# K's edges in four parts, V's image stored inside the column loop, and half of the rotated Q behind the first scores

## The chip, the cores and the metric

The kernel runs on one core of a Trainium2 chip. The metric is the device time of one execution in microseconds, of which the lower is the better; the time of a kernel is the median of several executions. A core has five engines that run their own instruction streams and wait for one another by semaphores: TensorE (PE: matmuls and transposes into PSUM, with weight loads on PEld), VectorE (DVE), ScalarE (ACT), POOL (GpSimd) and SP (SyncE), which here only issues DMAs. PSUM has eight banks of 512 floats in each of 128 partitions.

## The reference

Input x is (1, 128, 40, 40), float32. Cut to what matters:

```
x = x + conv(layernorm over channels of x)          # "conv" is windowed attention, below
t = tokens of x                                     # 1600 x 128
t = t + moe(layernorm(t))                           # t_n + sum of 2 of 8 experts, gelu MLPs 128-128-128

conv(x):  q, k, v = split(x @ w_qkv.T + b_qkv);  q = q / 4;  8 heads of 16 channels
    k_w, v_w = for each pixel its 17 x 17 window of k and of v (zeros outside), C*289 numbers
               per pixel, read as 289 vectors of 128, that is (289, 8 heads, 16)
    attn = softmax(q . k_w) * mask;  out = attn . v_w;  return out @ w_proj.T + b_proj
```

The window's C*289 numbers are laid out channel after channel and then read as 289 rows of 128, so a vector of 16 numbers that a head multiplies with q mostly lies within one channel's window, runs along it, and sometimes crosses from one channel to the next.

## The kernel before

**Stages.** The first 65 us prepare: layernorm, the matmuls for K, Q and V, their images (`kimg`, `vimg`: 40 x 40 with a frame), and several rearranged copies through DRAM. Then comes the column loop (65 to 318 us), one iteration for each of the 40 image columns x, and after it the projection, the router and the experts (318 to 436 us).

**One column.** POOL multiplies the rotated Q with a band (`spread(x)`, into `wb`): these are the weights for `scores(x)` on TensorE, three groups into banks 0 to 2, each of four tiles, against K's turned slab `kt` and its half-swapped copy `kh`. Each group ends with a small matmul that adds the boundary terms `inj` (the vectors that cross channels). VectorE's `shift(x, g)` takes the minimum and adds the mask, ScalarE's `exps(x)` exponentiates, TensorE's `turn_probs(x)` transposes, VectorE's `weigh(x)` masks, TensorE's `products(x)` multiplies with V's skewed slab `sv`, and VectorE's `pick_out(x)`, `pick_sum(x)` take the result. TensorE's iteration i is scores(i), turn_probs(i-1), products(i-2).

**What a column needs made ahead.** VectorE's `turn(x)` makes `kt` for column x from `zt`, in iteration x-2, ScalarE's `half_blocks(x)` the `kh` from it. The boundary terms: POOL's `boundary_mul(x)` multiplies Q (`qb` and `xln`, chunks of four columns, loaded by 15 small DMAs in four groups, `q_load(c, g)`) with `dkx`, VectorE's `boundary_add(x)` sums, POOL's `boundary(x)` spreads to `inj`. In POOL's iteration i the order is spread(i+1), mask(i), boundary_mul(i+3), boundary(i+1). `dkx` is the difference of two pieces of K's image in DRAM: `edges_in` loads them to `gk`, `edge_difference` on VectorE subtracts. V's slab: ScalarE's `slab(x)` copies it from `vimg` to `uv`, SP's `store(x)` writes it to DRAM (484.5 KB), SP's `load(x)` reads it back skewed (539.5 KB) to `sv`. K's four slabs went the same way before the loop: `zslab(n)`, `zk_store(n)`, `zk_load(n)`, then TensorE's `zturn(n)` transposes them, ScalarE's `zt_copy(n)` copies them out. slab(0) and slab(1) use the buffers `uv` that zk_store(2) and (3) read.

**The rotated Q.** `q_turn(k)`, k = 0 to 3, rotates ten columns of Q by 20 small matmuls of 40 columns (the profile counts a float32 matmul as two); `copy_q(k)` on VectorE and `half_of_q(k)` on ScalarE copy the result from bank `QRB[k]` to `qrot` and `qhalf`, which spread(10k) to spread(10k+9) read.

**Order.** All orders are written out by hand, by the code's own order on each engine. SP is one queue: an instruction that waits holds up all behind it.

## Time and profile before

| | us |
|---|---|
| three runs | 436.99, 438.38, 438.93 |
| their median | 438.38 |
| the profiled execution's own time | 437.91 |
| its span | 436.1 |
| busy in it: TensorE | 401.2 (92%) |
| VectorE | 302.0 (69%) |
| ScalarE | 280.2 (64%) |
| POOL | 210.1 (48%) |

The span is the profiled execution from the first to the last instruction; the time has 1.8 us more around it. Busy times are sums over stages that differ in what holds them up, so a share says little about what a change in one stage is worth; the rows below are taken from the stage that is changed. The granted clock of TensorE is 0.945 on the mean of the span.

### The profile page before, as it was taken

To read this page: it belongs to the slowest core of one execution; us is meant where nothing else is said; L and a number is where in the kernel's file an instruction comes from. 1 tells how busy PE (TensorE), PEld (TensorE's weight loads), DVE (VectorE), ACT (ScalarE), POOL (GpSimd) and SP (SyncE) were. 2 spreads that over 40 slices of the span, in tenths; PEclk is the share of its full clock that TensorE was granted. 3 is DMA by queue.
4 is the path that set the end of the run, shared out by engine and by line. 5 is a ranking of instruction groups with operands and counts; after the bars stand their busy time and mean duration, and the time that the engine had idled before them with its cause. 6 is when DMAs were issued, how large, how long until landed. Compare 5 with 4: busy or idle time off the path is not lost.

```text
span 436.1 us, 16839 instructions
## 1 busy us (share of the span) xinstructions
PE 401.2 (92%) x7070; PEld 281.3 (64%) x7070; DVE 302.0 (69%) x765; ACT 280.2 (64%) x495; POOL 210.1 (48%) x268
## 2 busy tenths in 40 slices
PE   4899969599999998999999999999689978999997
PEld 2779955377777676777776776777455544465553
DVE  1351366499999899999988888999465746516323
ACT  2260659698899998999999889677322442253232
POOL 9901161666666565657667667675288030001000
PEclk9695558899999999999999999999899999999999
DMA  6179877866767666566667665446965000000500
GB/s 174 62 245 300 204 210 263 315 197 195 229 209 234 204 213 194 185 219 226 218 173 234 177 213 200 148 158 197 233 217 139 2 0 2 0 20 0 172 19 19
DMA packets 35049, 72.17 MB, mean 165 GB/s; under 512 B 8052, under 2 KB 22029, under 8 KB 34157
## 3 DMA queue, kind: packets, MB, share of 16 engines
q1 hardware_dynamic: 33851, 69.41, 50.2%
q8 instruction: 56, 0.92, 0.9%
q0 software_dynamic: 144, 1.32, 0.8%
q10 hardware_dynamic: 979, 0.36, 0.3%
q14 instruction: 19, 0.16, 0.1%
HBM read 42.24 MB, written 28.84 MB: 163 GB/s over the span
## 4 chain that ended last, share of the span: by engine, by line
PE 77%; DVE 6%; DMA 6%; ACT 5%; issue 3%; SPq 2%; DVEq 0%; ACTq 0%
PE ps L1001 22%; PE ps L1024 10%; PE ps L1046 9%; PE ps L1006 7%; DMA zsl<-uv 5%; PE ps L1165 4%; PE ps L1212 4%; PE ps L1027 3%; PE ps L1032 3%; PE ps L1107 2%; SPq L357 1%; PE ps L1179 1%; PE ps L918 1%; PE ps L1058 1%; DVE prb L1490 1%
## 5 line engine op out<-in xcount | busy, mean ns | idle before, releaser
L1001 PE MATMUL ps<-slabs 128*32 128x401 f32 x528 | 118.2, 512 | 10.5 <-ACT prb L778 4.9
L1001 PE MATMUL ps<-prb,slabs 128*32 128x401 f32 x494 | 114.0, 515 | 0.6 <-issue 0.6
L1413 DVE CUSTOM_DVE_ANT_0 scn<-ps,con 128x401 f32<-128x401 f32 x120 | 65.0, 571 | 21.8 <-PE ps L1006 21.5
L787 ACT ACTIVATE exb<-scn,lowest 128x401 f32<-128x401 f32 x120 | 74.2, 621 | 4.7 <-DVE lowest L1413 4.7
L1006 PEld LDWEIGHTS ps<-con,slabs 128*32 128x32 f32 x960 | 42.5, 112 | 48.1 <-issue 47.7
L588 POOL TENSOR_TENSOR slabs<-con,qrot 128x192 f32<-128x192 f32 (+4 forms) x67 | 30.5, 459 | 83.4 <-DVE slabs L1403 75.8
L1403 DVE COPY_PREDICATED slabs<-con,zt 128x1152 f32<-128x1152 int32 x41 | 67.2, 1640 | 0.1
L1006 PE MATMUL ps<-con,slabs 128*32 128x128 f32 x960 | 60.6, 275 | 0.2 <-issue 0.2
L776 ACT ACTIVATE prb<-slabs 64x1169 f32<-64x1169 f32 x40 | 47.2, 1179 | 12.6 <-DVE slabs L1403 11.9
L1024 PE MATMUL ps<-con,exb 128*128 128x128 f32 x360 | 48.8, 280 | 3.6 <-issue 3.3
L1046 PE MATMUL ps<-pm,slabs 128*32 128x78 f32 (+19 forms) x2720 | 49.0, 221 | 0.6 <-issue 0.3
L723 ACT ACTIVATE uv<-vimg 128x969 f32<-128x969 f32 x40 | 41.3, 1034 | 10.2 <-DMA zsl<-uv 9.3
L1046 PEld LDWEIGHTS ps<-pm,slabs 128*32 128x32 f32 x2720 | 46.2, 113 | 1.4 <-issue 1.3
L1024 PEld LDWEIGHTS ps<-con,exb 128*128 128x128 f32 x360 | 39.2, 142 | 11.6 <-issue 10.9
L595 POOL TENSOR_TENSOR slabs<-con,sbd 128x384 f32<-128x384 f32 x40 | 41.8, 1046 | 4.1 <-DVE sbd L1388 4.1
L778 ACT ACTIVATE prb<-slabs 64x1041 f32<-64x1041 f32 x40 | 42.9, 1073 | 1.0
L1001 PEld LDWEIGHTS ps<-slabs 128*32 128x32 f32 x528 | 32.9, 111 | 12.7 <-issue 11.2
L612 POOL TENSOR_TENSOR xt<-xln,wide 120x600 f32<-120x600 f32 x20 | 29.8, 1488 | 7.0 <-DMA xln<-qd 7.0
L1388 DVE TENSOR_REDUCE sbd<-xt 120x40 f32<-120x600 f32 x40 | 30.5, 762 | 0.0
L1001 PEld LDWEIGHTS ps<-prb,slabs 128*32 128x32 f32 x494 | 29.0, 111 | 1.3 <-issue 1.3
L612 POOL TENSOR_TENSOR xt<-qb,wide 120x600 f32<-120x600 f32 x18 | 28.0, 1553 | 1.5 <-DMA qb<-qd 1.5
L588 POOL TENSOR_TENSOR slabs<-con,kimg 128x192 f32<-128x192 f32 (+4 forms) x63 | 28.3, 455 | 0.0
(175 smaller groups left out, 696.9 us busy)
## 6 DMA issues: line engine op xcount, KB each, us to landing
slabs<-zsl SPq DMA_DIRECT2D x40, 539.5 KB
zsl<-uv SPq DMA_DIRECT2D x44, 484.5 KB, 3.9
ebs<-zsl SPq DMA_DIRECT2D x4, 539.5 KB, 5.2
vimd<-vimg SPq DMA_DIRECT2D x1, 1612.0 KB, 6.8
xt<-x_in SPq DMA_DIRECT2D x8, 200.0 KB, 7.1
slabs<-combd SPq DMA_DIRECT2D x1, 1600.0 KB, 6.6
kimd<-prb SPq DMA_DIRECT2D x1, 1596.0 KB
con<-ctab POOLq DMA_DIRECT2D x1, 1288.0 KB, 6.0
```

Of the source, the lines that this page charges most:

```text
L588: gp.tensor_tensor(v((wb, wsplit)[dst][x & 1], TW * (a - d0), (2 * TW, n), (8, 4), (1, 8)), cv("band", (8, n), (K, 4), (1, 8), off=BOFF - ...
L595: gp.tensor_tensor(v(inj[x & 1], 0, (8, KH), (1, 8)), cv("hot_of", (0, KH), (1, 8)), v(sbd, x * YP, (1, KH), (1, 8)), ALU.mult).then_inc(S ...
L612: gp.tensor_tensor(v(kprod[x % 3], 0, (1, NCC), (NCC, SZ), parts=n), v(qb[c & 1], xi * SZ, (XE, NCC), (1, SZ), parts=n), v(dkx, x * SZ, (S ...
L776: nc.scalar.activation(v(a, 0, (1, KTW), parts=HB), v(b, 0, (1, KTW), parts=HB, p0=HB), ACT.Copy).then_inc(S["kh_copied"], 1)
L778: nc.scalar.activation(v(a, 0, (1, KTW - C), parts=HB, p0=HB), v(b, C, (1, KTW - C), parts=HB), ACT.Copy).then_inc(S["kh_copied"], 1)
L787: nc.scalar.activation(v(ex[x & 1], a, (1, NC3)), v(scn, (x & 1) * NB * NC3 + a, (1, NC3)), ACT.Exp, scale=-1.0, bias=lowest[:, NB * (x & ...
L1001: mm(bank(g, (1, NC3), parts=TW, p0=TW * i), w, v((kt, kh)[b & 1][x & 1], b // 2 * C, (1, NC3)), start=first, stop=False, skip_group_check ...
L1006: return mm(bank(g, (1, C), parts=TW, p0=TW * i), v(inj[x & 1], t * TW, (1, TW)), cv("unperm", (1, C)), start=False, stop=True, skip_group ...
L1024: nc.tensor.transpose(bank(3 + lw, (8, HC), (7, 8), off=C * g + 7), v(ex[x & 1], g * NC3 + lw * C, (1, C)), cv("ident", (1, C)))
L1046: last = mm(bank(6, (1, NPS * (z - a)), off=NPS * a, parts=TW, p0=TW * i), v(sv[x & 1], u * C + TW * i, (1, TW)), v(pm[x & 1], at0, (PW - ...
L1403: last = nc.vector.copy_predicated(v(kt[x & 1], 0, (C, NU), (1, C)), cv(name, (9, NU), (1, C), off=(1 - C - ph) % K).bitcast(I32), v(zt, a ...
L1413: nc.vector.tensor_tensor_reduce(v(scn, i * NC3, (1, NC3)), bank(g, (1, NC3)), cv("pos"), 1.0, 3e38, ALU.add, ALU.min, lowest[:, i:i + 1]) ...
```

## The change

It does five things. (1) K's edges are loaded and subtracted in four parts (`GXS`: columns 0 to 20 as before, then three times 11) instead of two; parts 1 to 3 are issued by SP in its iterations 1, 12 and 23 and subtracted by VectorE in its iterations 3, 14 and 25, and POOL waits for the part that each boundary_mul reads. Their buffers are now in `kimg` and `prb`. (2) V's image goes to DRAM (1612.0 and 403.0 KB) in SP's iteration 8 (`PAD`), not before the loop. (3) SP's line before the loop is woven anew: zk_store(2) comes right after the first edges, q_load(1, 0) ahead of zk_load(2), and load(0) no longer waits for all edges. (4) q_turn(2) and q_turn(3), with their copies, come behind the first scores, ahead of zturn(2), which now waits for them; `QRB` gives q_turn(1) to (3) the banks 3, 6 and 7. (5) ScalarE has zslab(3) ahead of its two q_loads and slab(0) ahead of zt_copy(0).

```
-GX0 = 21
+GXS = (0, 21, 32, 43, 54)
-QRB = (0, 1, 2, 3)
+QRB = (0, 3, 6, 7)
+        for a, z in zip(GXS[1:-1], GXS[2:]):
+            gk.append([v(kimg, SZ * YP, (1, (z - a) * (PS + 1))), v(prb, 2 * KTW, (1, (z - a) * (PS + 1)))])
...
             edges_in(sp, 0)
+            zk_store(2)
             zk_load(1)
             q_load(sp, 0, 0)
             q_load(sp, 0, 1)
-            edges_in(sp, 1)
-            zk_store(2)
             zk_store(3)
-            zk_load(2)
             q_load(sp, 1, 0)
-            zk_load(3)
-            q_load(sp, 1, 1)
...
             def load(x):
                 sp.wait_ge(stored[x & 1], 16 * (x // 2 + 1))
-                if x < 2:
-                    sp.wait_ge(S["dk_ready"], 2)
-                else:
+                if x >= 2:
                     sp.wait_ge(S["av_done"], x - 1)
...
             store(0)
+            zk_load(2)
+            q_load(sp, 1, 1)
             store(1)
+            load(0)
             q_load(sp, 1, 2)
-            load(0)
+            zk_load(3)
             load(1)
             q_load(sp, 1, 3)
-            sp.wait_ge(S["v_copied"], NQ)
-            images_out(sp, vimg, vimd, S["vim_out"])
             for i in range(SZ):
...
+                for p in range(1, len(GXS) - 1):
+                    if i == GXS[p] - 20:
+                        if p == 1:
+                            sp.wait_ge(S["zslab"], NZK)
+                        else:
+                            sp.wait_ge(S["dk_ready"], p)
+                        edges_in(sp, p)
+                if i == PAD:
+                    sp.wait_ge(S["v_copied"], NQ)
+                    images_out(sp, vimg, vimd, S["vim_out"])
...
                 pool.wait_ge(S["kmul"], x)
+                pool.wait_ge(S["dk_ready"], sum(a < x + NCC for a in GXS[:-1]))
...
             boundary(1)
-            pool.wait_ge(S["dk_ready"], 2)
...
             zslab(2)
+            zslab(3)
             q_load(act, 0, 2)
             q_load(act, 0, 3)
-            zslab(3)
...
+            slab(0)
             zt_copy(0)
             half_blocks(0)
             half_of_q(0)
+            slab(1)
             zt_copy(1)
-            slab(0)
-            slab(1)
-            for k in range(1, NQ):
-                half_of_q(k)
+            half_of_q(1)
             half_blocks(1)
...
                 exps(i)
                 if i == 0:
+                    half_of_q(2)
+                    half_of_q(3)
                     zt_copy(2)
                     zt_copy(3)
...
             def q_turn(k):
                 pe.wait_ge(S["qy_copied"], NQ)
-                pe.wait_ge(S["v_copied"], QRB[k] + 1)
+                pe.wait_ge(S["v_copied"], NQ)
+                if k >= 2:
+                    pe.wait_ge(S["zt_copied"], k + 1)
...
-            for k in range(1, NQ):
+            for k in range(1, 2):
                 q_turn(k)
...
                             pe.wait_ge(S["zt_copied"], 3)
-                            pe.wait_ge(S["qr_copied"], NQ)
-                            pe.wait_ge(S["qhalf_copied"], 2 * NQ)
...
                 if i == 0:
+                    q_turn(2)
+                    q_turn(3)
+                    pe.wait_ge(S["qr_copied"], NQ)
+                    pe.wait_ge(S["qhalf_copied"], 2 * NQ)
                     zturn(2)
                     zturn(3)
...
             copy_q(0)
-            edge_difference(1)
-            for k in range(1, NQ):
-                copy_q(k)
             boundary_add(1)
...
             dve.wait_ge(S["kh_zero"], 2)
+            copy_q(1)
             turn(1)
...
                         shift(i, g)
+                if i == 0:
+                    copy_q(2)
+                    copy_q(3)
                 if i + 2 < SZ:
                     turn(i + 2)
                 if 0 <= i - 1 < SZ:
                     weigh(i - 1)
+                for p in range(1, len(GXS) - 1):
+                    if i == GXS[p] - 18:
+                        edge_difference(p)
```

On ScalarE, from the third K slab to the second half_blocks, before the change stand these rows: the slab copies (`uv`), its last DMA issue, zt_copy (`slabs`, `zt`), half_blocks (`prb`) and half_of_q (`kimg`).

```order
L723 ACTIVATE uv<-kimg 128x969
L357 DMA qb<-qd 56x1x160
...
L357 DMA qb<-qd 8x160
L723 ACTIVATE uv<-kimg 128x969
L757 ACTIVATE slabs<-ps 128x512 x4
L757 ACTIVATE slabs<-ps 128x128 x2
L776 ACTIVATE prb<-slabs 64x1169
L778 ACTIVATE prb<-slabs 64x1041
L765 ACTIVATE kimg<-ps 64x10x40 x2
L757 ACTIVATE zt<-ps 128x512 x2
L757 ACTIVATE zt<-ps 128x128
L723 ACTIVATE uv<-vimg 128x969 x2
L765 ACTIVATE kimg<-ps 64x10x40 x6
```

And the same stretch after it, up to the first row of the second half_blocks:

```order
L729 ACTIVATE uv<-kimg 128x969 x2
L358 DMA qb<-qd 56x1x160
...
L358 DMA qb<-qd 8x160
L729 ACTIVATE uv<-vimg 128x969
L763 ACTIVATE slabs<-ps 128x512 x4
L763 ACTIVATE slabs<-ps 128x128 x2
L782 ACTIVATE prb<-slabs 64x1169
L784 ACTIVATE prb<-slabs 64x1041
L771 ACTIVATE kimg<-ps 64x10x40 x2
L729 ACTIVATE uv<-vimg 128x969
L763 ACTIVATE zt<-ps 128x512 x2
L763 ACTIVATE zt<-ps 128x128
L771 ACTIVATE kimg<-ps 64x10x40 x2
```

Both K slabs now stand ahead of the DMA issues, V's slab 0 ahead of the first zt_copy, and of the six later half_of_q rows two are left here.

On TensorE the rows from the first zturn (`ps<-con,ebs`, 128x128) to the first group of scores(0), before the change; `ps<-ebs,con` with 40 columns is q_turn, ten instructions a chunk.

```order
L972 MATMUL ps<-con,ebs 128x128 x9
L962 MATMUL ps<-ebs,con 128x40 x10
L972 MATMUL ps<-con,ebs 128x128 x9
L962 MATMUL ps<-ebs,con 128x40 x30
L1001 MATMUL ps<-slabs 32x401
```

After it, the same place and then the end of scores(0) with what follows it:

```order
L981 MATMUL ps<-con,ebs 128x128 x9
L971 MATMUL ps<-ebs,con 128x40 x10
L981 MATMUL ps<-con,ebs 128x128 x9
L971 MATMUL ps<-ebs,con 128x40 x10
L1008 MATMUL ps<-slabs 32x401
...
L1013 MATMUL ps<-con,slabs 32x128 x4
L971 MATMUL ps<-ebs,con 128x40 x20
L981 MATMUL ps<-con,ebs 128x128 x18
L1008 MATMUL ps<-slabs 32x401
```

Twenty of the forty rotation matmuls have moved from ahead of scores(0) to between it and the 18 transposes of zturn(2) and (3), which scores(1) follows.

## Rows read from the trace of the kernel before

**Rows 1.** Timeline of PE: start, length, rows within columns 0 to 8

```profile
42.16 4.33 PE L962 MATMUL ps<-ebs,con 128*128 128x40 f32 x20
...
65.40 0.85 PE L1001 MATMUL ps<-slabs 128*32 128x401 f32 x1 [4.30 <-ACT kimg L765]
...
69.54 1.64 PE L972 MATMUL ps<-con,ebs 128*128 128x128 f32 x13
...
72.35 0.50 PE L1001 MATMUL ps<-slabs 128*32 128x401 f32 x1
...
75.17 1.20 PE L1024 MATMUL ps<-con,exb 128*128 128x128 f32 x9
...
81.94 0.84 PE L1001 MATMUL ps<-slabs 128*32 128x401 f32 x1 [4.86 <-ACT prb L778]
...
89.15 0.50 PE L1001 MATMUL ps<-slabs 128*32 128x401 f32 x1
...
117.53 0.50 PE L1001 MATMUL ps<-slabs 128*32 128x401 f32 x1 [0.17 <-issue]
```

**Rows 2.** Timeline of POOL: boundary(0), boundary_mul(4), boundary(2)

```profile
54.77 1.02 POOL L595 TENSOR_TENSOR slabs<-con,sbd 128x384 f32<-128x384 f32 x1
...
79.25 1.46 POOL L612 TENSOR_TENSOR xt<-xln,wide 120x600 f32<-120x600 f32 x1 [6.42 <-DMA xln<-qd]
80.66 1.02 POOL L595 TENSOR_TENSOR slabs<-con,sbd 128x384 f32<-128x384 f32 x1
```

**Rows 3.** Chain that ended last, in order of time, before scores(0)

```profile
48.36 11.65 DMA zsl<-uv
60.03 1.99 ACT uv L723 x2
```

**Rows 4.** DMA issues of slab stores: KB each, us to landing

```profile
zsl<-uv SPq DMA_DIRECT2D x44, 484.5 KB, 3.9
```

**Rows 5.** Timeline of SP's issues: first q_loads, second edges, last q_load(1), V's image

```profile
40.04 6.53 SPq L357 DMA_DIRECT2D qb<-qd  x8
46.61 0.85 SPq L345 DMA_DIRECT2D exb<-kimd  x1
...
73.11 1.92 SPq L357 DMA_DIRECT2D xln<-qd  x3
...
75.47 1.83 SPq L330 DMA_DIRECT2D vimd<-vimg  x1
```

**Rows 6.** Timeline of ACT: its q_loads, half_of_q(0), the end of half_blocks(3)

```profile
38.57 5.69 ACTq L357 DMA_DIRECT2D qb<-qd  x7
...
52.57 1.03 ACT L765 ACTIVATE kimg<-ps 64x400 f32<-64x400 f32 x2 [2.59 <-DVE qrot L1372]
...
80.63 1.07 ACT L778 ACTIVATE prb<-slabs 64x1041 f32<-64x1041 f32 x1
```

**Rows 7.** Timeline of DVE: boundary products, copy_q(0), edge difference, boundary_add(3), shift(3), shift(6)

```profile
49.24 2.22 DVE L1460 TENSOR_TENSOR xt<-qb,wide 120x600 f32<-120x600 f32 x2 [3.69 <-DMA qb<-qd]
...
51.98 0.56 DVE L1372 COPY qrot<-ps 128x400 f32<-128x400 f32 x1
58.53 1.53 DVE L1379 TENSOR_TENSOR wide<-exb,slabs 120x1320 f32<-120x1320 f32 x1 [5.99 <-DMA slabs<-kimd]
...
78.72 0.76 DVE L1388 TENSOR_REDUCE sbd<-xt 120x40 f32<-120x600 f32 x1
...
91.11 0.56 DVE L1413 CUSTOM_DVE_ANT_0 scn<-ps,con 128x401 f32<-128x401 f32 x1
...
109.19 0.57 DVE L1413 CUSTOM_DVE_ANT_0 scn<-ps,con 128x401 f32<-128x401 f32 x1
```

**Rows 8.** Windows: busy us by engine, granted clock, DMA share, GB/s

```profile
28.00:31.00 3.00, 3.00 (x30) 3.00 (x28) 1.07 (x2) 1.66 (x3) 0.00 (x0) 1.00 1.13 375
34.00:35.00 1.00, 1.00 (x7) 1.00 (x7) 0.00 (x0) 0.00 (x0) 0.00 (x0) 0.50 0.94 386
40.00:46.00 6.00, 5.82 (x28) 5.82 (x28) 1.16 (x2) 1.64 (x3) 2.22 (x3) 0.50 0.93 242
```

More of the change, by code:

```diff
@@ L250, in program @@
         kprod = [xt[:, i * NCC * SZ:(i + 1) * NCC * SZ] for i in range(3)]
-        gk = [[v(scn, i * GX0 * (PS + 1), (1, GX0 * (PS + 1))) for i in range(2)],
-              [v(exb, 0, (1, GX - GX0 * (PS + 1))), v(sv[0], 0, (1, GX - GX0 * (PS + 1)))]]
+        gk = [[v(scn, i * GXS[1] * (PS + 1), (1, GXS[1] * (PS + 1))) for i in range(2)]]
+        for a, z in zip(GXS[1:-1], GXS[2:]):
+            gk.append([v(kimg, SZ * YP, (1, (z - a) * (PS + 1))), v(prb, 2 * KTW, (1, (z - a) * (PS + 1)))])
         wq2, wqr, wk, wv, wp = sb("wq2", 2 * C), sb("wqr", C), sb("wk", C), sb("wv", C), sb("wp", C)
@@ L296, in program @@
         skewv = [sem(f"skewv{i}") for i in range(2)]
-        gk_in = [sem(f"gk_in{i}") for i in range(2)]
+        gk_in = [sem(f"gk_in{i}") for i in range(len(GXS) - 1)]
         q_in = [sem(f"q_in{i}") for i in range(2)]
@@ L340, in edges_in @@
         def edges_in(eng, part):
-            a, n = ((0, GX0), (GX0, NX - GX0))[part]
+            a, n = GXS[part], GXS[part + 1] - GXS[part]
             for dst, row in zip(gk[part], (2 * HC + 1, 0)):
@@ L1375, in edge_difference @@
             def edge_difference(part):
-                a, z = ((0, GX0), (GX0, NX))[part]
+                a, z = GXS[part], GXS[part + 1]
                 n = 8 * NCC
```

## The prediction

> **What bounds the kernel now.** I read the page, then the timeline of each engine up to column 8, the chain of waits, SP's and POOL's waits, and windows for clock and DMA. From column 3 on TensorE works through: scores(3) starts at 89.15 and scores(8) at 117.53, 5.68 us a column [rows 1]. So the end moves with the moment at which the columns reach this pace, and the change works on what lies before it. There the reader is to see four things.
>
> First, scores(0) starts at 65.40 after 4.30 us idle [rows 1], although its first operands are ready: boundary(0), its last own one, ends at 54.77 + 1.02 = 55.79 [rows 2]. It waits for all four chunks of the rotated Q, whose last copies stand on ScalarE behind slab(0) and slab(1), and these waited until 60.03 for the store of K's third slab, issued at 48.36 and 11.65 us under way [rows 3], where such a store takes 3.9 as a rule [rows 4]. It stood behind K's second edges, issued from 46.61 [rows 5].
>
> Second, scores(2) starts at 81.94 after 4.86 idle. The row blames ScalarE's half_blocks, which ends at 81.70 [rows 1, 6]. But that is half_blocks(3), which scores(2) doesn't need; what scores(2) needs is boundary(2) on POOL, 80.66 + 1.02 = 81.68 [rows 2]. POOL had waited 6.42 us to 79.25 for chunk 1 of the Q that the boundary products read [rows 2]; its last piece was issued at 73.11 to 75.03 [rows 5]. This is the stall whose cause has to be seen rightly.
>
> Third, VectorE is as full as TensorE in columns 3 to 7: shift(3) at 91.11, shift(6) at 109.19, 6.03 a column [rows 7]. scores(8) starts 117.53 - 109.19 = 8.34 after shift(6) [rows 1, 7], the length of the way turn, spread, boundary_mul, boundary on two engines. An early TensorE will run into this way.
>
> Fourth, the clock. In 28 to 31 us TensorE is at 1.00 of 2.4 GHz; in 34 to 35 at 0.50 (1.2 GHz), though busy in every us of both [rows 8]: what it did between is the stream of 40-column matmuls alone.
>
> **The change, step by step.** SP now issues zk_store(2) right after the first edges, at 37.1 instead of 48.36, so the chunk 0 loads stand behind 484.5 KB more. At 242 to 375 GB/s [rows 8] that is 2.0 to 1.3 us if they are served in order; 0 if the queue has room by then. I take 1.6, since the DMA share in 40 to 46 is 0.93 [rows 8]: there is hardly room.
>
> 1. Chunk 0 is used at 49.24 + 1.6 = 50.8 [rows 7]. From there to boundary(0)'s end it takes 55.79 - 49.24 = 6.55 (two products, an add, copy_q(0), half_of_q(0), spread, boundary) [rows 2, 7], and 0.2 to the matmul: scores(0) at 57.6, 7.8 earlier. ScalarE is no later. zslab(3) now stands ahead of its seven DMA issues: the store it waits for has landed by 39.6, so they begin at 40.6, not 38.57, and take 5.69 to 46.3 [rows 6]. What followed them before, zslab(3), zt_copy(0) and half_blocks(0), was over at 52.57 - 2.59 = 49.98 [rows 6], 5.7 after their end; now slab(0), as long, stands in zslab(3)'s place: 52.0, and copy_q(0) ends only at 54.1 [rows 7]. The store behind slab(0) lands near 46.5, being only behind the first edges. The second edges no longer hold VectorE, which idled 5.99 before them [rows 7].
>
> 2. scores(0) at half clock as now, 69.54 - 65.40 = 4.14 [rows 1]: to 61.8.
>
> 3. New between scores(0) and zturn(2): q_turn(2) and q_turn(3), 20 matmuls each. At full clock 0.10 each (30 in 3.00 us [rows 8]), 2.0 a chunk; at half 4.33 [rows 1]. I take full: 65.8. Then copy_q(3) 0.56 [rows 7] and half_of_q(3) 1.03 (the same kind that ScalarE starts at 52.57, between its neighbours) [rows 6] with TensorE waiting, since zturn(2) reuses banks 6 and 7: 67.6. Before, these 8.6 us lay ahead of scores(0), beside the waiting; the cover is gone. On VectorE turn(2) and boundary_add(2) are queued behind the two copies, on ScalarE zt_copy(2) to half_blocks(2) behind half_of_q(3); they wait 2 to 3 us, but scores(1) needs none of them and scores(2) comes late enough.
>
> 4. zturn(2) and (3), 18 transposes: 13 take 1.64 at full clock [rows 1], so 2.3 to 2.8; at half 4.4. The clock will have fallen: after scores(0) come 40-column matmuls and an idle stretch. 4.4: scores(1) at 72.0. Before it was 72.35 [rows 1]. **The 7.8 us are nearly all spent again here.**
>
> 5. scores(1) at half clock 4.4, turn_probs(0) 1.9 (75.17 to 81.94 - 4.86 = 77.08 [rows 1]): 78.3, 1.2 later than now.
>
> 6. Stall two. SP issues chunk 1's first pieces at 47, the last after load(1), which waits for the landing of store(1): 56 + 3.9, so issues about 61 to 63, landing by 67 (73.11 to 79.25 now [rows 2, 5]). POOL needs it for boundary_mul(4), which with boundary(2) takes 81.68 - 79.25 = 2.4 [rows 2], so until 75.9 its landing is hidden. scores(2) starts at 78.3, not 81.94, and at full clock.
>
> 7. From turn_probs(0) VectorE is the longest: weigh(0) and boundary_add(3), which took from 77.08 to 78.72 + 0.76, 2.4 [rows 1, 7], then a column of 6.03: shift(3) at 86.7, against 91.11: **4.4 earlier**.
>
> 8. The new edge differences stand in VectorE's columns 3, 14 and 25, each a third of the 1.53 [rows 7], 0.5. In column 3 it is on the path (VectorE is full, and scores(8) stands 8.34 behind shift(6)); in 14 and 25 TensorE alone sets the pace. -0.5. POOL's new waits for parts cost nothing: part 1 is needed by boundary_mul(7), whose column the difference precedes, and its loads are issued 10 us before.
>
> Sum: 4.4 - 0.5 = 3.9. The profiled execution took 437.91, 0.47 under the median of the three runs (438.38): 434.0 beside it, **434.4** beside the median.
>
> **The images in the loop.** V's store (1.6 + 0.4 MB) goes out in column 8, where SP's slab traffic runs. At 375 GB/s it holds the queue for 5.4 us; its second issue takes SP 1.83 [rows 5, 8]. store(11) is queued behind it, and ACT's slab(13) waits for that: it may be 2 x 5.65 - 1.0 = 10.3 us under way. Ahead of it stand load(8) and the images, with itself 0.54 + 2.0 + 0.48 = 3.04 MB, 8.1 us at 375, and some 1 us of late issue: 9.1. Cost nothing, by 1.2 us; the load for products(9) has a like slack.
>
> **The rivals.**
> *TensorE stays at full clock over steps 3 to 5.* scores(0) brings the clock up, and the 40-column matmuls behind it and the 1.8 us of idleness don't take it down before scores(1). Half clock in 34 to 35, while busy throughout [rows 8], speaks against; that before it came up with scores(0) and stayed up for zturn(2), (3) and scores(1) [rows 1] speaks for it. Then the zturns take 2.8 and scores(1) 2.8 [rows 1], 3.2 less: gain 7.1, 431.3. The Trainium skill (TensorE: Matmul & The Clock Gate, Why this matters for your kernels) is on this rival's side: it tells one to keep TensorE busy without a break to get and hold the full clock, and by that the 40-column matmuls would count as work; the row of 34 to 35 doesn't agree. Chance 0.15.
>
> *Another wait takes stall two's place.* The last pieces of chunk 1 now stand behind two slab stores, three loads and the landing of store(1). If they land at 79 as now, scores(2) stands at 81.9 as now, TensorE and VectorE catch up a little, and 0.5 goes to the edge difference: gain 0 to 1, 437.4 to 438.4. The like comes of half clock in q_turn(2) and (3), which costs 4.7: about 0.8 slower than now in the sum, less what VectorE has in hand. For it: SP's queue has been late twice already [rows 2, 3]. Against: 1.8 MB of edges and 2 MB of image no longer stand in it. Chance 0.18.
>
> *Slower: the image store stalls columns 10 to 12.* Should the queue carry only the 242 GB/s of 40 to 46 [rows 8], the 3.04 MB take 12.6 us and store(11) is 13.6 under way, 3.3 over; load(9), the same again, stops TensorE itself. Two waits of 3.3 make 6.6: 441.0. It decides from some 10.3 us under way. Against: stores, loads and images drew 375 before. Chance 0.08.
>
> The forecast as it stands: 0.59.
>
> **How the numbers follow.** The likeliest case's own range is 432.4 to 436.2: 1.6 for chunk 0 and 0.4 for a shorter half-clock stretch one way, 0.4 for chunk 0 and 1.4 for a part of q_turn(3) and its turns at half clock the other. The whole range takes in most of the full-clock case and, of the other wait, what still gains 1: 430.9 to 437.5. Half a per cent, 2.2 us, is what a measurement of this kernel can tell. Faster by more: 0.15, and 0.55 of the 0.59, so 0.70; within: 0.18 and the remaining 0.04, so 0.22; slower 0.08.
>
> **What would show it.** Right: scores(0) near 57.6, scores(1) still near 72, no stall before scores(2), shift(3) near 87, half clock somewhere in 62 to 76; ScalarE's slab(0) near 46.5; SP's images in column 8 with no idle of ScalarE before slab(13). Wrong: scores(1) before 70.5 (gain larger), POOL waiting for xln<-qd beyond 70 (gain gone), or any DMA wait in columns 9 to 13.

## The result, and the profile after

| | median, us | lowest to highest | runs |
|---|---|---|---|
| before | 438.87 | 436.47 to 443.29 | 20 |
| changed | 443.22 | 438.38 to 447.20 | 20 |

The ratio is 1.0064, 95% interval 1.0034 to 1.0094: slower by 0.64%, 2.8 us. (The ratio leaves disturbed runs out, so it is not the quotient of the two medians, which lie 4.35 us apart.) 434.4 was forecast, 430.9 to 437.5 as range; the result lies outside, on the other side of no change. The profiled execution took 442.71 us, its span is 440.9, 4.8 longer than that of before.

The timeline of TensorE in the changed kernel, at the places that [rows 1] show of before:

```profile
57.84 0.85 PE L1008 MATMUL ps<-slabs 128*32 128x401 f32 x1 [2.10 <-POOL slabs L601]
...
63.01 5.99 PE L971 MATMUL ps<-ebs,con 128*128 128x40 f32 x40
70.78 4.08 PE L981 MATMUL ps<-con,ebs 128*128 128x128 f32 x18 [1.78 <-issue]
74.78 0.88 PE L1008 MATMUL ps<-slabs 128*32 128x401 f32 x1
...
86.72 0.50 PE L1008 MATMUL ps<-slabs 128*32 128x401 f32 x1 [0.87 <-POOL slabs L601]
...
133.04 0.33 PE L1039 MATMUL ps<-con,exb 128*32 128x46 f32 x10 [1.56 <-issue]
139.36 1.20 PE L1031 MATMUL ps<-con,exb 128*128 128x128 f32 x9 [2.22 <-issue]
145.04 0.52 PE L1008 MATMUL ps<-prb,slabs 128*32 128x401 f32 x1 [1.15 <-issue]
```

scores(0) stands at 57.84, as forecast (57.6). The 40 rows of q_turn(2) and (3) take 5.99, not 4.0, and scores(1) comes at 74.78, 2.8 later than forecast and 2.4 later than before. Then, in its iterations 10 to 12, TensorE idles three times for something that the profile calls issue: it waits there for no semaphore that the profile shows. Before had 0.61 and 0.33 of this in the same stretch.

VectorE, the first shift of columns 3, 4 and 8 with the edge difference of column 3, which answer to [rows 7], and of column 39:

```profile
88.23 0.57 DVE L1424 CUSTOM_DVE_ANT_0 scn<-ps,con 128x401 f32<-128x401 f32 x1
...
93.28 0.59 DVE L1390 TENSOR_TENSOR wide<-kimg,prb 120x440 f32<-120x440 f32 x1
...
94.98 0.57 DVE L1424 CUSTOM_DVE_ANT_0 scn<-ps,con 128x401 f32<-128x401 f32 x1
...
119.28 0.57 DVE L1424 CUSTOM_DVE_ANT_0 scn<-ps,con 128x401 f32<-128x401 f32 x1
...
311.00 0.57 DVE L1424 CUSTOM_DVE_ANT_0 scn<-ps,con 128x401 f32<-128x401 f32 x1
```

POOL's boundary_mul(4), with no DMA wait now [rows 2], and its longest wait for a Q piece, in column 25; then its waits for DMAs in 85 to 310 us, grouped: total, times, longest:

```profile
72.09 1.47 POOL L619 TENSOR_TENSOR xt<-xln,wide 120x600 f32<-120x600 f32 x1
...
223.58 1.49 POOL L619 TENSOR_TENSOR xt<-xln,wide 120x600 f32<-120x600 f32 x1 [2.93 <-DMA xln<-qd]
```

```profile
POOL xt L619 <- DMA xln<-qd: 3.2, 2, 2.9
POOL xt L619 <- DMA qb<-qd: 2.1, 2, 1.6
```

SP's issues in columns 8 and 23: the image, the store and the Q pieces behind it; the last part of the edges and the Q pieces behind that:

```profile
122.88 1.26 SPq L330 DMA_DIRECT2D vimd<-vimg  x1
124.18 0.43 SPq L331 DMA_DIRECT2D vimd<-vimg  x1
125.70 0.32 SPq L323 DMA_DIRECT2D zsl<-uv  x1
126.06 6.60 SPq L358 DMA_DIRECT2D qb<-qd  x4
...
215.50 0.87 SPq L346 DMA_DIRECT2D kimg<-kimd  x1
216.42 0.85 SPq L346 DMA_DIRECT2D prb<-kimd  x1
...
217.91 2.35 SPq L358 DMA_DIRECT2D xln<-qd  x3
```

Four Q issues behind the image take SP 6.60 us, where eight take 6.53 in [rows 5]. Read by the start of the first shift of a column, against before: shift(3) 88.23 to 91.11, **2.9 earlier**; shift(8) 119.28 to 121.22, 1.9 earlier; shift(13) 151.41 to 149.06, **2.3 later**; shift(26) 229.09 to 224.84, 4.3 later; shift(39) 311.00 to 306.50, 4.5 later. So the start did gain. The lead is still 1.9 at shift(10) and a lag of 2.3 at shift(13): these three columns took 4.3. Up to shift(25) the lag stays at 2.4, and the one column from there to shift(26), in which POOL waits its 2.93, adds 1.9.

### The profile page after: what moved, and what is told of

Its sections match the earlier page's. It is cut to its first block, busy times and chain, and to the rows that moved or that the text cites. A ratio compares the mean times of both kernels' runs of the same rounds, so it can differ in the third digit from the quotient of the medians.

```text
span 440.9 us, 16880 instructions
## 1 busy us (share of the span) xinstructions
PE 405.4 (92%) x7070; PEld 282.5 (64%) x7070; DVE 302.4 (69%) x767; ACT 281.1 (64%) x495; POOL 213.8 (48%) x268
## 4 chain that ended last, share of the span: by engine, by line
PE 71%; DVE 10%; issue 7%; POOL 3%; DMA 3%; ACT 2%; SPq 2%; DVEq 0%; POOLq 0%; ACTq 0%
PE ps L1008 18%; PE ps L1031 8%; PE ps L1053 7%; PE ps L1013 5%; PE ps L1172 4%; PE ps L1219 4%; PE ps L962 3%; PE ps L1034 3%; PE ps L1114 2%; PE ps L1039 2%; POOL slabs L601 2%; DVE slabs L1414 1%; SPq L358 1%; PE ps L971 1%; PE ps L1186 1%
## 5 line engine op out<-in xcount | busy, mean ns | idle before, releaser
L1414 DVE COPY_PREDICATED slabs<-con,zt 128x1152 f32<-128x1152 int32 x41 | 68.3, 1666 | 1.4 <-ACT zt L763 1.3
L1013 PE MATMUL ps<-con,slabs 128*32 128x128 f32 x960 | 61.8, 276 | 0.5 <-issue 0.5
L601 POOL TENSOR_TENSOR slabs<-con,sbd 128x384 f32<-128x384 f32 x40 | 44.7, 1116 | 1.6 <-DVE sbd L1399 1.6
L594 POOL TENSOR_TENSOR slabs<-con,kimg 128x192 f32<-128x192 f32 (+4 forms) x63 | 29.5, 476 | 0.0
L619 POOL TENSOR_TENSOR xt<-qb,wide 120x600 f32<-120x600 f32 x18 | 26.9, 1492 | 2.8 <-DMA qb<-qd 2.1
## 6 DMA issues: line engine op xcount, KB each, us to landing
vimd<-vimg SPq DMA_DIRECT2D x1, 1612.0 KB, 7.4
```

Source lines behind the costliest of these rows:

```text
L594: gp.tensor_tensor(v((wb, wsplit)[dst][x & 1], TW * (a - d0), (2 * TW, n), (8, 4), (1, 8)), cv("band", (8, n), (K, 4), (1, 8), off=BOFF - ...
L601: gp.tensor_tensor(v(inj[x & 1], 0, (8, KH), (1, 8)), cv("hot_of", (0, KH), (1, 8)), v(sbd, x * YP, (1, KH), (1, 8)), ALU.mult).then_inc(S ...
L619: gp.tensor_tensor(v(kprod[x % 3], 0, (1, NCC), (NCC, SZ), parts=n), v(qb[c & 1], xi * SZ, (XE, NCC), (1, SZ), parts=n), v(dkx, x * SZ, (S ...
L1013: return mm(bank(g, (1, C), parts=TW, p0=TW * i), v(inj[x & 1], t * TW, (1, TW)), cv("unperm", (1, C)), start=False, stop=True, skip_group ...
L1414: last = nc.vector.copy_predicated(v(kt[x & 1], 0, (C, NU), (1, C)), cv(name, (9, NU), (1, C), off=(1 - C - ph) % K).bitcast(I32), v(zt, a ...
```

## The experiments

All times are medians; each group of runs has its own runs of before on its chip, and the ratios are to these. A difference of two ratios is uncertain by 0.4 to 0.7%, 2 to 3 us, so most of the differences below are each hardly larger than their uncertainty, and means over several pairs say more than one pair. A single trace shows one execution, so places are read from traces and prices from ratios.

### The parts of the change apart

```
image early (1)               -                if i == PAD:
                              -                    sp.wait_ge(S["v_copied"], NQ)
                              -                    images_out(...)
     and before the loop      +            images_out(...)            behind q_load(sp, 1, 3)
all q_turns ahead (2)         -QRB = (0, 3, 6, 7)
                              +QRB = (0, 1, 2, 3)
     q_turn, copy_q, half_of_q +            for k in range(1, NQ):    ahead of the loop, none in it
last edges early (3)          -                    if i == GXS[p] - 20:
                              +                    if i == (None, 1, 12, 20)[p]:
```

e1_images_early is the changed kernel with edit 1:

> The changed kernel, with V's image stored before the column loop again (behind q_load(1, 3)), the rest of the change kept. Theory A: in column 8 the 2.0 MB of image hold up the fetch of TensorE's own instructions; the three stalls put down to 'issue' at 131.5, 137.1 and 143.9 (1.56 + 2.22 + 1.15 us) go, though a stall of some 1 to 2 us may stay, since the kernel before has one there too; the image goes out in the idle stretch of the DMA queue at 64 to 72 us at no cost. Time 443.2 - 4 = 439. Rival B: the image in column 8 costs nothing, as I forecast, and those stalls come of something else: 443. Rival C: the image costs its time wherever it stands, since the early loads queue behind it: scores(2) late again, 441 to 443.

e2_q_ahead has edit 2:

> The changed kernel, with all four chunks of the rotated Q ahead of scores(0) again, as before the change. Theory A: the two chunks behind scores(0) cost 6.0 us of TensorE, a wait for their copies of 1.8 and a fall of the clock, all on the path to scores(1), while ahead of scores(0) they would be done at about 64.5; then scores(0) at about 66, scores(1) at about 72.8 at full clock against 74.78 at half, turn_probs(0) ends at 77.5 against 80.15: 2.5 less, 440.7. Rival B: they do what they are for, scores(0) 8 us later pushes all back: 445 or more. Rival C: later columns take up any difference: 443.

e3_images_alone is the kernel before with its image moved into SP's iteration 8:

> The kernel before, with one thing of the change: V's image stored in SP's iteration 8. Theory A (TensorE's instructions are fetched late behind the image): stalls put down to issue in columns 10 to 12, 438.9 + 3.5, less up to 1 that columns 2 and 3 gain without the image at 75 us: 441.4 to 442.4. Rival B (the image is hidden there): 438 to 439, with no such stall beyond the 2 us that the kernel before has.

e4_all_three has edits 1, 2 and 3:

> The changed kernel with three things altered: V's image before the loop, all of the rotated Q ahead of scores(0), and the last part of K's edges issued in SP's iteration 20 instead of 23, where it stood ahead of the last piece of a Q chunk for which POOL then waited 2.93 us. Theory A (three separate losses of 4, 2.5 and 2): 443.2 - 8.5 = 434.7, faster than the kernel before by 1%. Rival B (the losses cover one another, or TensorE is held by something else): 437 to 439.

e5_edge3_early has edit 3:

> The changed kernel with one edit: the last part of K's edges is issued in SP's iteration 20, not 23, so it no longer stands ahead of the last piece of a Q chunk. Theory: this piece was late in the changed kernel (POOL waited 2.93 us at 223.58) and the column from shift(25) to shift(26) took 7.7 us; with the edit the POOL wait shrinks below 1 us and that column takes 6.2 to 6.7, so 1 to 1.5 us of the loss come back: span near 439.5, median 441.5 to 442.5. Rival (the column is long because of the edge difference on VectorE itself and of TensorE's own stall, the Q piece is hidden): that column still takes 7.3 or more and the median stays near 443.

| | median | ratio, interval | shift(3) | shift(39) |
|---|---|---|---|---|
| e1_images_early | 440.26 | 1.0000 [0.9948, 1.0052] | 86.9 | 306.5 |
| e2_q_ahead | 440.76 | 1.0081 [1.0043, 1.0119] | 86.1 | 310.9 |
| e3_images_alone | 441.53 | 1.0065 [1.0023, 1.0107] | 90.6 | 310.5 |
| e4_all_three | 438.24 | 0.9992 [0.9955, 1.0029] | 86.0 | 305.1 |
| e5_edge3_early | 441.97 | 1.0033 [1.0003, 1.0064] | 86.1 | 307.9 |

Edit 1 takes 0.64% off (uncertain by 0.6), and the issue waits of iterations 10 to 12 with it; put alone into the kernel before, the image costs 0.65%, as expected, and brings such waits. In the timeline of TensorE in e3_images_alone the first of these three stands ahead of the image, which SP issues at 125.47 there, so that one is not its doing; the two others follow it:

```profile
124.58 0.40 PE L1047 MATMUL ps<-pm,slabs 128*32 128x57 f32 x19 [1.11 <-issue]
135.97 0.33 PE L1033 MATMUL ps<-con,exb 128*32 128x46 f32 x10 [0.72 <-issue]
142.31 2.18 PE L1025 MATMUL ps<-con,exb 128*128 128x128 f32 x9 [2.21 <-issue]
```

e2 brings nothing by its ratio, where its theory had 2.5 us, though its shift(3) is 2.1 earlier. Of its lead of 5.0 over before it loses 2.8 up to shift(11), beside a wait of POOL for a Q piece of 2.59, then 4.1 in the next column, beside an issue wait of 3.06, and 2.4 between shift(25) and shift(26). And e1, without the issue waits, is no faster than before, though it leads by 4.2 at shift(3): 3.4 of it go up to shift(11), beside waits for the Q chunks of columns 8 to 11 and 12 to 15, and 2.1 between shift(25) and shift(26), where the last edges stand ahead of a Q piece. e4, with all three edits, is as fast as before too, as its rival had it (437 to 439, for 434.7 by the theory of three separate losses). First TensorE's waits for POOL in e1, four times, where the changed kernel has three and 1.6 us, then POOL's for Q pieces in e1 and in e4:

```profile
PE ps L1007 <- POOL slabs L600: 4.6, 4, 1.8
```

```profile
101.00 1.48 POOL L618 TENSOR_TENSOR xt<-qb,wide 120x600 f32<-120x600 f32 x1 [1.89 <-DMA qb<-qd]
125.42 1.49 POOL L618 TENSOR_TENSOR xt<-xln,wide 120x600 f32<-120x600 f32 x1 [2.30 <-DMA xln<-qd]
```

```profile
100.19 2.69 POOL L618 TENSOR_TENSOR xt<-qb,wide 120x600 f32<-120x600 f32 x1 [2.02 <-DMA qb<-qd]
124.05 1.48 POOL L618 TENSOR_TENSOR xt<-xln,wide 120x600 f32<-120x600 f32 x1 [1.82 <-DMA xln<-qd]
```

SP issues the last piece of a chunk in the iteration just ahead of the one in which POOL uses it, whatever the time. When the columns start earlier, the pieces are what is late next. e5 came out about as expected: POOL's wait at the last edges fell from 2.93 to 0.27, and the column from shift(25) to shift(26) from 7.7 to 6.9 us, where 6.2 to 6.7 was expected. The ratio is 0.31%, 1.4 us, lower, which is within its uncertainty of 0.43.

### How the image costs

```
e6   +                if i in (8, 10, 12, 14, 16):     32 partitions of the image each time
e7   +                    for a in range(0, IMGP, w):  four column slices of 3.2 KB a row
e8 (before, once more)
     +                if i == 20:
     +                    sp.wait_ge(S["vim_out"], 16 * 2)
     +                    images_out(sp, vimg, vimd, S["vim_out"])
```

> The changed kernel, with V's image in five pieces of 32 partitions (0.40 MB each) in SP's iterations 8, 10, 12, 14 and 16 instead of all in 8. Theory A (TensorE's instruction fetch is late behind a long backlog of the DMA engines): no piece makes a backlog, the issue stalls of columns 10 to 12 (4.9 us in the changed kernel's trace) shrink to the 1 to 2 that the kernel before has: 439.5 to 440.5. Rival B (the bytes cost their time wherever they go in the loop): 443.

> The changed kernel, with V's image still in column 8 and as many bytes, but cut by columns into four stores with packets of 3.2 KB, like those of the slabs, instead of one with 12.9 KB. Theory A1 (it is the length of the backlog that holds up the instruction fetch): the same issue stalls of 4 to 5 us, 443. Theory A2 (it is the long packets: a fetch waits for one or two on each engine): the stalls go, 439 to 440.

> The kernel before, with V's image stored a second time in SP's iteration 20 (the same data to the same place, 2.0 MB more of work that nothing needs). Theory A: as in column 8, issue stalls of TensorE of 3 to 4 us within two to four columns, here 22 to 24: 438.9 + 3.5 = 442.4. Rival B (column 8 is special, since TensorE and VectorE are both full there): under 1 us, 439.5.

| | median | ratio, interval |
|---|---|---|
| e6_image_pieces | 445.44 | 1.0171 [1.0124, 1.0218] |
| e7_image_slices | 441.74 | 1.0027 [0.9981, 1.0073] |
| e8_image_twice | 443.34 | 1.0071 [1.0030, 1.0113] |

The second image of e8 costs 0.71% in a place with nothing else new, and a wait moves with it. Of the 3 to 4 us of issue waits that were expected there only this one is in its trace, which shows an execution of 439.81 us, faster than the median (timeline of TensorE):

```profile
203.97 0.98 PE L1049 MATMUL ps<-pm,slabs 128*32 128x63 f32 x48 [1.68 <-issue]
```

Five pieces, spread over ten columns, were the slowest kernel of all (439.5 to 440.5 was expected), with issue waits nearly as long as with the whole image, behind the second piece, issued at 135.49. Behind the third to fifth there is none over 0.53:

```profile
141.84 0.52 PE L1010 MATMUL ps<-prb,slabs 128*32 128x401 f32 x1 [1.76 <-issue]
148.31 0.26 PE L1055 MATMUL ps<-pm,slabs 128*32 128x27 f32 x9 [1.70 <-issue]
```

This speaks against my first theory, that the length of the backlog in SP's queue makes TensorE wait. With slices of 3.2 KB in place of rows of 12.9 KB no issue wait in columns 8 to 13 is longer than 0.20, but POOL waits for Q pieces instead:

```profile
123.19 1.49 POOL L623 TENSOR_TENSOR xt<-xln,wide 120x600 f32<-120x600 f32 x1 [1.67 <-DMA xln<-qd]
...
148.92 2.36 POOL L623 TENSOR_TENSOR xt<-qb,wide 120x600 f32<-120x600 f32 x1 [3.34 <-DMA qb<-qd]
```

The time of e7 lies between its two cases (443, and 439 to 440): 0.37% under the changed kernel, uncertain by 0.55. So only its trace tells long rows from long backlogs. Nor are e6 and e7 clean tests, since late Q pieces stand beside the image in both: POOL waits 8.1 and 10.6 us for them in 85 to 310 us, in the changed kernel 5.3. With the Q pieces early they weren't run.

An account that fits is that long rows hold up the transfers that bring TensorE its own instructions. The page of the profile counts such a queue (packets, MB, share of 16 engines' span), alike before and after:

```profile
q8 instruction: 56, 0.92, 0.9%
```

The Trainium skill (Runtime: NRT & Kernel Launch, Instruction fetch mechanics) states that a sequencer fetches its instructions in blocks of 16 KiB by a DMA queue of its own, and (DMA: Bandwidth & Descriptors, Queues, rings and completion order) that a DMA engine goes from one queue to another only at the end of a packet. By the first of these the fetch is mostly hidden; if the waits of 1.56, 2.22 and 1.15 are fetches, beside the image it was not, but no view here shows which transfer TensorE waits for, and none shows the order in which a DMA engine serves its queues. What the traces show is that the longest issue wait in iterations 10 to 13 is 1.20 to 3.06 in each of the eight kernels that store the image in long rows from iteration 8 on, and 0.20 in e7. The mechanism behind them is argued from e7, not shown, and e6 is left unexplained.

### The Q chunks one iteration earlier

```
-                    c, g = divmod(i + 7, XC)
-                if i and c < NXC:
+                    c, g = divmod(i + 8, XC)
+                if c < NXC:
```

e9_best is e4 with this edit; e10_q_loads_alone the kernel before with it; e11_best_q_behind is e9 without edit 2, e12_best_image_in_loop is e9 without edit 1, and e15_changed_q_loads is the changed kernel with this edit alone.

> The kernel e4_all_three with each piece of the Q chunks loaded one SP iteration earlier. In e4 POOL waited 2.0, 1.8 us and more for such loads (chunks 2 and 3), and by column 10 half of the 5 us of lead at column 3 was gone. Theory D (the loads' cadence, tied to the columns, takes back what the start gains): the waits go, shift(8) at 116 instead of 118, 438.2 - 2 = 436, below the kernel before by 0.7%. Rival E (VectorE's 6.0 us a column takes it back anyway): 438.

> The kernel before with one edit: every Q chunk from the third on is loaded one iteration of SP earlier. Theory (the chunk loads matter only where the start of the loop has been made earlier; before the change they are landing in time, POOL waits 0.28 us for one at 218.54): no difference, 438 to 439, ratio within 0.003 of 1. Rival (the best kernel so far owes its gain to this edit alone): 435.5 to 436.5, ratio 0.994, and columns 3 to 11 take less than the 46.3 us of before.

> The changed kernel with the image stored before the loop, the last edges in SP's iteration 20 and the Q chunks one iteration earlier, but with the third and fourth rotation chunk behind the first scores, as changed. Against the kernel that has them ahead of the first scores (436.06) it tells what this move alone is worth. Theory: scores(1) is 2.1 us later (q_turn(2) and (3) cost 6.0 there and their copies 1.8), shift(3) at 87 to 88 instead of 86.2, and with no later wait to swallow it the median is 0.7 to 2 us higher: 436.8 to 438. Rival (VectorE, not TensorE, holds columns 3 to 7 and catches this up): 436, no difference.

> The best kernel so far (436.06) with V's image stored in SP's iteration 8 instead of before the loop. Theory: the store of the image holds up TensorE's instructions whatever the rest does; columns 11 to 13 lose 3.5 to 4.5 us to idle time that ends with issue: 439.5 to 440.5. Rival (the image hurt only because it met late Q pieces and edges): at most 1 us, 436 to 437.

> The changed kernel with one edit: every Q chunk from the third on is loaded one iteration of SP earlier. Theory: the waits of POOL for Q pieces (5.3 us in columns 3 to 39 of the changed kernel) go, and with them the column after shift(25), about 2 us: 440.5 to 441.5, ratio 1.002; the image stays in its place and its 3.5 to 4.5 us with it, so it stays 3.5 to 5 us behind the kernel before with the same edit (436.24). Rival (the image and the late Q pieces hurt only together): 438 or less.

| | median | ratio, interval | shift(3) | shift(39) |
|---|---|---|---|---|
| e9_best | 436.06 | 0.9940 [0.9911, 0.9968] | 86.2 | 304.9 |
| e10_q_loads_alone | 436.24 | 0.9912 [0.9882, 0.9943] | 89.6 | 302.5 |
| e11_best_q_behind | 436.60 | 0.9939 [0.9912, 0.9967] | 84.9 | 301.8 |
| e12_best_image_in_loop | 438.70 | 0.9954 [0.9923, 0.9985] | 85.7 | 307.8 |
| e15_changed_q_loads | 437.82 | 0.9964 [0.9916, 1.0011] | 87.6 | 306.2 |

The edit is worth 0.88% in the kernel before, 1.0% in the changed one, 0.52% between e4 and e9. My theory said that it would bring nothing to the kernel before, since that had only 2.1 us of such waits; this was wrong. In e10 POOL's waits in 85 to 310 us have no DMA left among them:

```profile
POOL slabs L588 <- DVE slabs L1403: 70.0, 36, 3.5
POOL mx L602 <- DVE pm L1438: 5.2, 6, 3.4
```

e10 against e9 and e11 is the sharpest finding of this group: with the edit, the unchanged start is as fast as the changed one, although that leads by 4.7 us at shift(3) (84.9 to 89.6). In e11 the lead is 4.1 at shift(12), 2.2 at shift(22), 0.4 at shift(26). It goes in 12 to 16 and in 22 to 26. SP issues the edges in its iterations 12 and 20 there and VectorE subtracts them in 14 and 25, so the losses stand near the edges, which made them the next suspect. e11 itself came out as its rival had it (no difference to e9), with shift(3) at 84.9 for the 87 to 88 of the theory. e15 came out as its rival had it (438 or less): the image seemed to cost less once the Q pieces were early, 0.25% against e11 (which also has edit 3), and 0.14% in e12 against e9, where the time lies between the two cases and the trace still has its waits:

```profile
132.16 0.33 PE L1038 MATMUL ps<-con,exb 128*32 128x46 f32 x10 [1.30 <-issue]
138.49 1.20 PE L1030 MATMUL ps<-con,exb 128*128 128x128 f32 x9 [2.22 <-issue]
```

### The edges inside the loop

Into e10 come two more loads of eleven columns of edges, and in e14 their subtraction too:

```
+                if i in (12, 20, SZ - 2):
...
+                        sp.dma_start(v(dst, ..., (1, 11 * (PS + 1)), parts=8 * NCC),
...
+                if i in (14, 25):
+                    dve.wait_ge(S["again"], 32 if i == 14 else 64)
+                    tt(v(ebs, 2 * L, (SZ, 11), (1, SZ), parts=8 * NCC), ..., ALU.subtract)
```

> The kernel before with its Q chunks loaded one iteration earlier (436.24, ratio 0.9912), plus two more loads of eleven columns of edges by SP in its iterations 12 and 20, into buffers that nothing reads (so they are extra work and change no result). Theory: the parts that the change loads inside the loop cost about 1 us each, by SP's line and the queue; then this kernel is 1.5 to 2.5 us slower than without them: 437.8 to 438.7, ratio about 0.996. Rival (their loads are hidden, what costs is the subtraction on VectorE or nothing at all): 436.2, ratio 0.991.

> The same with the two loaded parts also subtracted on VectorE in its iterations 14 and 25, into a place that nothing reads. Theory (the loads cost, TensorE alone sets the pace in these columns): as without the subtraction, within 0.5 us. Rival (VectorE holds the shift of the next column after any late column): 0.5 to 1.2 us more than without it.

e13 measured 439.67, ratio 1.0035 [1.0002, 1.0068]: 1.2%, 5.4 us more than e10, over twice what I expected. e14 measured 441.14, 1.0048 [1.0011, 1.0085]: the subtraction adds nothing that can be told. In its trace e13 is 2.0 us behind e10 already at shift(12), before it has issued anything extra, so not all of the difference between the two traces is the loads'. From shift(12) to shift(26) e13 takes 83.9 us, e10 79.8: 4.1 for the loads by this pair of traces. Two of the waits, in the timeline of TensorE in e13:

```profile
167.78 0.30 PE L1013 MATMUL ps<-con,slabs 128*32 128x128 f32 x2 [1.01 <-issue]
172.71 0.50 PE L1008 MATMUL ps<-slabs 128*32 128x401 f32 x1 [0.80 <-DVE slabs L1410]
```

The loads cost, then. They were issued in iteration 12, at 149.35, though, and these waits stand some 18 us behind, so the way from load to wait isn't shown.

The counter-test takes the edges out of the loop and leaves the changed start:

```
-GXS = (0, 21, 32, 43, 54)
+GXS = (0, 21, 54)
-            gk.append([v(kimg, ...), v(prb, ...)])
+            gk.append([v(t, 0, (1, (z - a) * (PS + 1))) for t in (exb, scn)])
             zk_store(3)
+            sp.wait_ge(S["dk_ready"], 1)
+            edges_in(sp, 1)
...
+            edge_difference(1)                       on VectorE, just ahead of its loop
```

e16_edges_ahead has this, edit 1 and the early Q chunks; e17 is e16 without edit 1; e18 is e16 with edit 2.

> The changed kernel with K's edges in two parts as before, both loaded and subtracted before the loop (the second issued by SP behind the store of K's last slab, subtracted by VectorE just ahead of the first shift), the image stored before the loop and the Q chunks one iteration earlier. So the changed start without image and edges in the loop. Theory (the edges in the loop eat the lead of the start: two extra parts cost 4.5 us in the kernel before): shift(3) at 86 to 88 and the lead over the kernel before with early Q chunks (89.6 there) reaches the end: 432.5 to 434.5, ratio 0.985 to 0.990. Rival (the lead is lost whatever is loaded, because VectorE and TensorE catch up): 436, ratio 0.994, as with the edges in the loop.

> The same with V's image stored in SP's iteration 8. Theory A (the image costs by itself, 2.8 us as in three comparisons): 2 to 4 us slower than with the image before the loop. Theory B (it costs only beside late Q pieces and edges; with early Q pieces it cost 0.6 and 1.1 us within 2): at most 1 us slower.

> The first of these three with all four rotation chunks ahead of the first scores, as before. Theory: with nothing to swallow it, what moving two chunks behind the first scores is worth shows: shift(3) 1 us earlier or later (it was 84.9 with them behind and 86.2 with them ahead, 88.2 and 86.1 without early Q chunks; it hangs on when the clock falls), so within 1.5 us of the first either way. Rival (the move is worth the 7.8 us by which scores(0) is earlier, or half of it): 4 us slower than the first.

| | median | ratio, interval | shift(3) | shift(39) |
|---|---|---|---|---|
| e16_edges_ahead | 433.91 | 0.9879 [0.9831, 0.9927] | 84.9 | 299.7 |
| e17_edges_ahead_image_in_loop | 437.06 | 0.9954 [0.9919, 0.9988] | 86.1 | 302.4 |
| e18_edges_and_q_ahead | 433.17 | 0.9854 [0.9806, 0.9902] | 86.6 | 300.5 |

e16 is 0.6% faster than e11, which has the edges in the loop (uncertain by 0.55); its 433.91 falls into the expected span. The image costs 0.75% again (theory A). And where the third and fourth rotation chunk stand makes no difference that can be told: 0.25% in favour of having them ahead, 0.01% between e9 and e11. e18, with edges, image and all rotation chunks ahead of the loop as before, is the fastest of all: 1.5% under before. TensorE's waits in 85 to 300 us, first e16, then e17:

```profile
PE ps L1002 <- issue: 0.8, 2, 0.5
PE ps L1033 <- issue: 0.5, 1, 0.5
PE ps L1047 <- issue: 0.2, 1, 0.2
```

```profile
PE ps L1034 <- issue: 1.4, 2, 1.2
PE ps L1003 <- issue: 0.9, 1, 0.9
PE ps L1003 <- POOL slabs L596: 0.9, 1, 0.9
```

## Why the prediction was wrong

**Right.** Step 1: scores(0) at 57.84 for 57.6; chunk 0 was used at 51.14 for 50.8. Step 6: the stall before scores(2) is gone, and the landing of chunk 1 stays hidden behind scores(1), as the cause given for it asked. The main reading of step 4 too: the 7.8 us are spent again ahead of scores(1).

**Mis-sized, steps 2 and 3.** scores(0) took 5.17 (57.84 to 63.01) for 4.14: the granted clock was 0.50 in its first 4.2 us, where before it was 0.50 in the first 2.6 and 0.93 in the next. And q_turn(2) and (3) took 5.99 for 4.0; the transposes of step 4 took 4.0 for 4.4. For the q_turns the windows of the changed kernel (columns as in [rows 8]) show why: the clock was full while most of them ran, 20 rows in the 2 us of 64 to 66, but fell to half for the last, while TensorE was busy, and stayed there until 76.

```profile
62.00:64.00 2.00, 2.00 (x25) 1.35 (x17) 1.17 (x6) 1.99 (x4) 1.95 (x2) 0.83 0.93 294
64.00:66.00 2.00, 2.00 (x20) 2.00 (x19) 0.51 (x1) 1.17 (x4) 0.00 (x0) 1.00 0.69 229
66.00:68.00 2.00, 2.00 (x13) 2.00 (x11) 0.07 (x1) 1.01 (x2) 0.00 (x0) 0.52 0.07 29
70.00:76.00 6.00, 5.22 (x26) 4.11 (x30) 1.62 (x2) 3.94 (x9) 3.50 (x4) 0.50 0.01 4
```

That set scores(1) 2.8 behind the forecast, and shift(3) 1.5 behind (88.23 for 86.7, 2.9 earlier than before in place of 4.4). But this is one execution. e5, the same program up to column 20, has

```profile
63.25 4.67 PE L971 MATMUL ps<-ebs,con 128*128 128x40 f32 x40
69.70 3.75 PE L981 MATMUL ps<-con,ebs 128*128 128x128 f32 x18 [1.78 <-issue]
```

and its shift(3) at 86.1. The changed kernel, e5, e6 and e7 are the same program up to column 8, and their shift(3) lies at 88.2, 86.1, 86.9 and 85.1, on the mean 86.6; 86.7 was forecast. The kernel before has such a spread too: e8 is the same program as it up to column 20, and its shift(3) is at 89.0, not 91.1. The error here didn't turn the sign.

**Failed: the images in the loop, "Cost nothing, by 1.2 us".** I followed the store behind the image and the load behind that, and for these the sum held: TensorE never waited for `sv`. Beside the image something else was late, TensorE's own issue: 1.56 + 2.22 + 1.15 = 4.9 us of idleness in the trace. By ratios the image costs 0.64, 0.65, 0.71, 0.75, 0.14 and 0.25% (e1, e3, e8, e17, e12, e15, each against its nearest twin; that of e15, e11, also has edit 3), on the mean 0.52%, 2.3 us. Trace and ratio don't go together pair by pair: e12 has 3.8 us of these waits and costs 0.14%, e17 has 2.1 and costs 0.75%. The rival that the image makes the kernel slower, with a chance of 0.08, had 441.0, 2.6 us above before, where 2.8 was measured; but it had another mechanism, waits for the stores and loads that never came, and a price of 6.6 for the image, so that its time came near is luck.

**Failed: step 8, the edges.** "In 14 and 25 TensorE alone sets the pace" and "POOL's new waits for parts cost nothing" hold as far as they go: e14 finds no price for the subtraction that can be told. What I never costed is the loads of parts 2 and 3, 3.4 us of SP and two transfers inside a line that before had none of them; only for part 1 did I look at the issue. They cost 1.2% (e13), 0.60% (e11 against e16), 0.86% (e9 against e18) and 0.10% (e15 against e17), on the mean 0.7%, 3 us; the last three have part 1 in it too. In the prediction they were counted as a removal ahead of the loop ("1.8 MB of edges and 2 MB of image no longer stand in it"), and not as an addition in it.

**The sum again.** The prediction's own sums hold but for roundings (438.38 - 3.9 is 434.5, and scores(0) would have ended at 61.7). What the start is worth, all else out of the way, is e16 and e18 against e10: 0.33 and 0.58%, 1.4 to 2.5 us, each uncertain by 0.57% (e18 is without the move of the rotation chunks); 3.9 was forecast for it, with 0.5 for the subtraction already taken off. With 3 us for the edges and 2.3 for the image this makes 2.8 to 3.9 slower; 2.8 was measured. The terms are each uncertain by 1 to 2 us, and they come from different kernels, so that they close so well is partly luck.

**Open.** By which way a store in the loop reaches TensorE's issue, by which way the loads of edges cost, why the image cost so little in e12 and e15, why five short pieces of the image were worse than one long, and why early Q chunks gave the kernel before 3.9 us where its trace shows 2.1 of waits for them.

## What to carry to other kernels

When a transfer is moved out of a crowded start into a loop, cost it there as well, every issue and every byte, and look in the trace not only at the engine that waits for it, but also at the waits marked issue. When a start is made earlier, look for what is tied to the iteration number, such as a load issued so many columns ahead: it becomes the next wait and eats the gain, and moving it one iteration may be worth more (here 0.9%) than the whole start (here 0.3 to 0.6%). And put the part that is to gain on a kernel without the parts that merely came with it: here the new start alone would have been a small gain at best, and in company it was a loss.

## What was not expected of the hardware

TensorE idled up to 3.06 us at a time (e2) with no semaphore to wait for that the profile shows, some 7 to 22 us after 2 MB in rows of 12.9 KB had been issued on another engine's queue. This came in the changed kernel, e2, e3, e5, e12, e15 and e17, behind iteration 20 in e8, and in no kernel that stored the image before the loop was there a wait of the kind over 0.61 us in iterations 10 to 13. But such waits aren't the image's alone: e14, with no image in its loop, has 1.31 and 1.11 at 98 and 115 us, before any of its extra loads, and e1 has 1.14 at 223. And TensorE's granted clock fell and rose at different places in executions of the same program: the 40 rows of q_turn(2) and (3) took 5.99 in the changed kernel and 4.67 in e5 and e11, and the level stood at half until 76.3 us in the changed kernel, but in e11 was back at full by 72, as its windows show:

```profile
66.00:68.00 2.00, 0.91 (x9) 0.77 (x7) 1.06 (x2) 0.80 (x2) 0.00 (x0) 1.00 1.00 423
...
72.00:74.00 2.00, 2.00 (x35) 1.00 (x37) 0.58 (x2) 1.98 (x5) 0.45 (x1) 1.00 0.03 8
```

Over the four kernels that are alike up to column 8, shift(3) differs by 3.1 us, more than most of the edits above are worth; the whole of it is there at shift(1) already, 73.57 us in e7 and 76.69 in the changed kernel.
